# Turning stage and recurrence as one stage, and an expert stage that loads its own outputs

## What is computed

```
h = layernorm(x)
h = h + attention(layernorm(h))          # 16 heads
h = h + experts(layernorm(h))            # 8 experts, each token goes to the best one
x = x + 0.5 * h

z = layernorm(x)                         # no weights
dxa = shifted_by_one_token(z) - z
xm  = z + dxa * miu_x
lora = tanh(xm @ A_lora)
w_in, k_in, v_in, r_in, g_in = z + dxa * (lambda + lora @ B_lora)      # five mixes
k, v, r = k_in @ Wk.T, v_in @ Wv.T, r_in @ Wr.T;  g = silu(g_in @ Wg.T)
w = td_miu + tanh(w_in @ td_A) @ td_B;  decay = exp(-exp(w))
S_t = decay_t * S_(t-1) + k_t v_t;  y_t = r_t (S_(t-1) + u k_t v_t)    # per head
x = x + (groupnorm(y) * g) @ Wo.T

x = x + 0.5 * (the same attention-and-experts block applied to layernorm(x))
```

## Time and profile before

| | us |
|---|---|
| median of 3 runs (lowest to highest) | 1484.05 (1483.67 to 1486.18) |
| the profiled execution, its own time | 1485.67 |
| span of that execution, first to last instruction | 1483.3 |
| VectorE busy | 1059.5 (71%) |
| ScalarE busy | 870.2 (59%) |
| GpSimd busy | 637.5 (43%) |

### The profile page before, as it was taken

The page is one execution under the profiler, slowest core; times in us unless marked ns, Lnnn a source line. Parts: engine busy times, 40 slices in busy tenths (PEclk is TensorE's granted clock), DMA queues, the critical chain, the costliest instruction groups (busy, mean ns, idle before and its releaser), DMA issues. The chain is left out here.

```text
span 1483.3 us, 39412 instructions
## 1 busy us (share of the span) xinstructions
PE 1245.7 (84%) x12592; PEld 705.4 (48%) x12593; DVE 1059.5 (71%) x1888; ACT 870.2 (59%) x1726; POOL 637.5 (43%) x733
## 2 busy tenths in 40 slices
PE   5699999999968496398898747799999999784893
PEld 3333334343358496144455444333433333284893
DVE  7789999999555232478888748899999999173232
ACT  5288888888821253444335325388888888620451
POOL 4313433344337464356766533324323433447462
PEclk9799999999965698599999858799999999965897
DMA  5513432221001221100000005311111111002124
GB/s 161 188 46 80 110 100 64 52 57 48 12 1 40 59 67 55 37 2 3 4 3 2 3 1 194 102 49 57 48 54 48 56 46 44 2 10 63 53 65 124
DMA packets 81640, 81.93 MB, mean 55 GB/s; under 512 B 16265, under 2 KB 53868, under 8 KB 81536
## 3 DMA queue, kind: packets, MB, share of 16 engines
q1 hardware_dynamic: 72704, 70.01, 17.1%
q0 software_dynamic: 4608, 8.44, 1.7%
q10 hardware_dynamic: 4224, 2.10, 0.5%
HBM read 50.56 MB, written 29.93 MB: 54 GB/s over the span
## 5 line engine op out<-in xcount | busy, mean ns | idle before, releaser
L868 DVE TENSOR_REDUCE maxima<-ps 128x2 f32<-128x1024 f32 x512 | 624.0, 1226 | 53.5 <-PE ps L701 43.9
L854 ACT ACTIVATE probs<-ps 128x512 f32<-128x512 f32 x1024 | 551.7, 596 | 77.6 <-PE ps L728 60.8
L701 PE MATMUL ps<-k_stack,q_stack 62*128 62x512 f32 x1024 | 388.4, 474 | 17.5 <-DVE maxima L868 11.1
L728 PE MATMUL ps<-q_stack,k_stack 64*128 64x512 f32 x1024 | 382.4, 460 | 0.1
L739 PE MATMUL ps<-probs,v_stack 128*32 128x256 f32 x4096 | 327.6, 392 | 1.3 <-ACT probs L854 1.2
L701 PEld LDWEIGHTS ps<-k_stack,q_stack 62*128 62x128 f32 x1024 | 157.9, 192 | 218.1 <-DVE maxima L868 132.7
L657 POOL TENSOR_TENSOR inv<-o_rows,minus_one 128x32 f32<-128x32 f32 x32 | 174.2, 5444 | 29.5 <-ACT o_rows L835 29.5
L728 PEld LDWEIGHTS ps<-q_stack,k_stack 64*128 64x128 f32 x1024 | 161.9, 186 | 13.2 <-ACT probs L854 6.6
L649 POOL CAST neg_wide<-maxima 128x16 fp32r<-128x16 f32 x64 | 12.6, 196 | 349.8 <-DVE maxima L868 349.8
L739 PEld LDWEIGHTS ps<-probs,v_stack 128*32 128x32 f32 x4096 | 81.0, 108 | 170.4 <-issue 121.9
L1348 POOL DMA_INDIRECT expert_out<-yt,number x80 | 78.2, 978 | 69.1 <-POOL number L1344 32.1
(11 more groups left out here) (204 smaller groups left out, 1686.6 us busy)
## 6 DMA issues: line engine op xcount, KB each, us to landing
q_stack<-q_split SPq DMA_DIRECT2D x256, 64.0 KB
k_stack<-k_split SPq DMA_DIRECT2D x512, 32.0 KB
q_split<-q_parts SPq DMA_DIRECT2D x16, 512.0 KB, 3.2
k_split<-k_parts SPq DMA_DIRECT2D x16, 512.0 KB, 4.2
xt<-sorted SPq DMA_DIRECT2D x80, 64.5 KB
w<-in_L_ffn_w SPq DMA_DIRECT2D x16, 256.0 KB, 3.0
rows<-expert_out SPq DMA_DIRECT2D x16, 256.0 KB, 4.3
x_all<-in_L_attn_x SPq DMA_DIRECT2D x8, 256.0 KB, 3.0
```

Source lines behind the costliest of these rows:

```text
L701: mm = t.matmul(psS[:, h, :], qs[g][score_rows(h), h // 2, u * P:(u + 1) * P], ks[g][score_rows(h), h // 2, :], start=True, stop=True)
L728: t.matmul(ring("e", u, n), ks[g][half(h), h // 2, u * P:(u + 1) * P], qs[g][half(h), h // 2, :], start=True, stop=True).then_inc(e_ready, 1)
L854: a.activation(probs[u % 2][:, h, :], ring("e", u, n), ACT.Exp, scale=float(DK) ** -0.5).then_inc(e_read, 1)
L868: v.tensor_reduce(maxima[i][:, :, pair, u:u + 1], psS[:, 2 * pair:2 * pair + 2, :], AX_X, ALU.max, negate=True).then_inc(s_read, 1)
```

## The change

The expert stage's SyncE, after its last load, waits for the scatters of all four rings and issues the eight loads of `ys` itself, inside the expert stage. The semaphores that count these loads now belong to the program, one set for each of the two blocks. The combining stage only adds and stores.

```diff
+                for i in range(RING):
+                    sp.wait_ge(y_stored[i], 16 * (SLOTS // RING))
+                for j in range(SL):
+                    here = slice(j * ST, (j + 1) * ST)
+                    sp.dma_start(y_all[:, here, :], tiles_of(ys)[:, here, :]).then_inc(y_loaded[j], 16)
```

```diff
+            @block.sync
+            def _(sp):
                 for x in signals:
-                    pool.sem_inc(x.sem, 1)
...
+                    sp.sem_inc(x.sem, 1)
+                sp.sem_inc(opened, 1)
...
+                v.tensor_scalar(s["gn_w_half"][:], s["gn_w"][:], 0.5, None, ALU.mult).then_inc(halved, 1)
+                v.tensor_scalar(s["gn_b_half"][:], s["gn_b"][:], 0.5, None, ALU.mult).then_inc(halved, 1)
+                add(0)
+                for j in range(STARTED):
+                    moments_of(j)
+                vec.wait_ge(halved, 2)
...
                 def next_xm(b, i):
+                    if isinstance(b, int) and b <= 2:
+                        vec.wait_ge(kept, b + 1 if b < 2 else SL)
...
+                        if opening(b):
+                            moments_of(STARTED + f)
...
                 def scan_start(b, i):
+                    if opening(b):
+                        vec.wait_ge(stores_set, 2 + len(state))
```

On GpSimd the constants and the 14 factor memsets come first, then three roots, then the zeros of the five tiles; a root follows each of batch 0's mixes:

```diff
+                gn.start(pool)
+                for x in q_factor + k_factor:
+                    g.memset(x[:], 1.0).then_inc(factors_set, 1)
+                pool.wait_ge(constants, 2)
...
+                for j in range(STARTED):
+                    root(j)
+                for x in [diag, aT] + state:
+                    g.memset(x[:], 0.0).then_inc(stores_set, 1)
...
+                        if opening(b):
+                            root(STARTED + f)
```

On ScalarE a slice's activations and the copy of the slice before follow a part of batch 0; on TensorE a turn does:

```diff
+                def further(b, j):
+
+                    if opening(b):
+                        apply(j)
+                        keep(j - 1)
+
+                apply(0)
+                apply(1)
+                keep(0)
+                apply(2)
+                keep(1)
...
                     a.activation(lora4[:], ps[0:LORA, 1, :], ACT.Tanh).then_inc(lora_kept.sem, 1)
+                    further(b, 3)
...
                 def mix_chain(b, i):
+                    if opening(b):
+                        keep(SL - 1)
+                        act.wait_ge(factors_set, 2 * LEVELS)
...
+                for j in range(STARTED):
+                    turn(j)
...
+                def turn_at(b, part):
+                    if opening(b):
+                        turn(STARTED + ("td", "rate", "k", "r", "g").index(part))
```

More of the change, by code:

```diff
@@ L1353, in _, with combine_phase @@
                     pool.wait_ge(y_stored[i], 16 * (SLOTS // RING))
-def combine_phase(nc, x_all, y_all, ys, out):
+def combine_phase(nc, x_all, y_all, y_loaded, out):
     with Phase(nc) as ctx:
-        y_loaded = [ctx.semaphore(f"y_loaded{j}") for j in range(SL)]
         added, stored = ctx.semaphore("added"), ctx.semaphore("stored")
@@ L1408 @@
 GN_EPS = 1e-5 * NH
[L1411 to L1488, removed]
-                    act.wait_ge(turned, j + 1)
-                    a.activation(zT[:, j:j + 1, 1:], ps[:, j % 2:j % 2 + 1, :], ACT.Copy).then_inc(kept, 1)
-                for j in range(SL):
-                    act.wait_ge(shift_ready, j + 1)
-                    if j >= 2:
-                        act.wait_ge(turned, j - 1)
-                    for q in range(ST):
-                        last = a.activation(normed[j % 2][:, q, :], x_all[:, j * ST + q, :], ACT.Identity,
-                                            bias=shift[j % 2][:, q:q + 1], scale=rstd[j % 2][:, q:q + 1])
-                    last.then_inc(normed_ready, 1)
-                    if j >= 1:
-                        keep(j - 1)
-                keep(SL - 1)
-            @block.tensor
-            def _(pe):
-                for j in range(SL):
-                    pe.wait_ge(normed_ready, j + 1)
-                    if j >= 2:
-                        pe.wait_ge(kept, j - 1)
-                    for q in range(ST):
-                        last = nc.tensor.transpose(ps[:, j % 2, q * P:(q + 1) * P], normed[j % 2][:, q, :], s["ident"][:])
-                    last.then_inc(turned, 1)
@@ L1880, in _, with turn @@
                 t = nc.tensor
+                def turn(j):
+                    pe.wait_ge(normed_ready, j + 1)
+                    if j >= 2:
+                        pe.wait_ge(kept, j - 1)
+                    for q in range(ST):
+                        last = t.transpose(ps[:, TURN_BANK + j % 2, q * P:(q + 1) * P], normed[j % 2][:, q, :], s["ident"][:])
+                    last.then_inc(turned, 1)
+                for j in range(STARTED):
+                    turn(j)
                 def project(b, bank, weights, f, made, rows=P):
@@ L1986, in scan_keys @@
                     k_next.wait(pe, b, LEVELS)
+                    if opening(b):
+                        pe.wait_ge(kept, SL)
                     x_added.free(pe, b)
@@ L2072, in ffn @@
             project_phase(nc, ps, s, x_all, z_all, rows, expert, first_row, xs)
-            expert_phase(nc, ps, s, expert, first_row, xs, ys)
-        ffn(load)
+            expert_phase(nc, ps, s, expert, first_row, xs, ys, y_all, y_loaded)
+        y_loaded = [[ctx.semaphore(f"y_loaded{n}_{j}") for j in range(SL)] for n in range(2)]
+        ffn(y_loaded[0], load)
         with ExitStack() as inner:
             zT = inner.enter_context(nc.sbuf_tensor("zT", [P, B, T + 1], F32))
-            turn_phase(nc, ps, s, x_all, y_all, ys, zT)
-            recurrence_phase(nc, ps, s, x_all, zT)
-        ffn()
-        combine_phase(nc, x_all, y_all, ys, out)
+            recurrence_phase(nc, ps, s, x_all, y_all, y_loaded[0], zT)
+        ffn(y_loaded[1])
+        combine_phase(nc, x_all, y_all, y_loaded[1], out)
 _INS = ['L0_attn_x', 'L0_ffn_w_proj', 'L0_ffn_ln1_w', 'L0_ffn_ln1_b', 'L0_ffn_ln2_w', 'L0_ffn_ln2_b',
```

102 lines of the change are left out of this document (78 added, 24 removed).

## The result

The changed kernel takes 1473.74 us (median of 4 runs, 1473.05 to 1475.03) against 1484.12 before (4 runs, 1483.67 to 1486.18): ratio 0.9934, 95% interval 0.9906 to 0.9963. That is 0.7 above the forecast of 1473.0 and inside its range. The profiled execution took 1475.03, its span is 1473.1, 10.2 less than before.

What follows compares the result with a forecast made beforehand. The first seam was taken as bound by latency, then ScalarE as the opening's bound; 7.7 - 0.2 + 3.5 = 11.0 gained from a median of 1484.05 gave 1473.0 us, range 1467 to 1479.

Steps and rivals of the forecast that it cites:

- Loads at the first seam: Between expert stage and first add: SyncE's issuing replaces GpSimd's drain as what the barrier awaits; first add near 592.3, 0.2 lost.
- End: Last scatter to span's end: loads issued earlier, eight adds run without a wait, stores end sooner; 3.5 gained, ends 2.5 and 4.2.
- Opening: First add to batch 1's first shift: 20.4 saved up to batch 0's first shift, part paid back; 7.7 gained.
- the paying back: Between first shifts of batches 0 and 1: five late slices lengthen the stretch from 16.84 to 29.5.
- The step that makes ScalarE the bound: Inside batch 0, behind a head of 4.2: ScalarE sets the pace with 20.9 of work, plus waits.
- Low clock through the opening: Rival: TensorE stays at 0.50 through the opening, the path ends 4.3 later; 1477.4 us, chance 0.12.
- the argument against it: Against the low clock: from the shifts on TensorE has some 8 us of work without a gap.
- Contention: In the opening: late slices' two-input VectorE adds slow beside GpSimd's mix; stretch between first shifts 30.2 with it, 28.9 without.
- "The overlap itself brings nothing": Opening: batch 0 after the last slice without barriers would start its LoRA matmul near 615.5, 8.5 earlier; the gain is the seam's.
- SyncE's drain: Rival at the barrier: this drain waits for its loads' data, 2.8 lost at the opening, 1.0 gained at the end; 1478.2, chance 0.06.
- the five round trips: Rival in batch 0: late slices' trips between engines stand in series, costing 34; 1494, chance 0.05; partly in series 1484, 0.05.
- the signs named: Trace landmarks: LoRA matmul near 604, ScalarE hardly a gap 616 to 640, batch 1's first shift near 641, last loads near 1454.

Runs made afterwards that it cites:

- e11: The changed kernel with one activation instead of four for each of the five late slices, leaving work out; 1465.66 us, one execution.
- e12: The changed kernel with VectorE making statistics of one tile instead of four of each late slice, leaving work out; 1469.51 us, one execution.
- e4: The changed kernel with five loads issued in front of the barrier and three behind it, at both seams; 1469.71 us against 1485.26 before.
- e1: The changed kernel with all eight slices turned ahead of batch 0, the stages still merged; 1465.72 us against 1485.26 before.
- e2: The changed kernel with SyncE issuing the eight loads behind the barrier again, at both seams; 1472.63 us against 1485.26 before.

## Why the prediction was right, and where it was not

- **Loads at the first seam**, 0.2 lost: 0.3 gained. The mechanism was right to the row: SyncE's issuing took the place of GpSimd's drain, and the drain of SyncE is 0.12. The term missed mainly because the issues took 5.66 where 5.99 was put in. That number varies from 5.2 to 6.5 between executions. The first add at 591.64 lies 0.66 from the 592.3 named, a little outside the 0.5 that was allowed.
- **End**, 3.5 gained: 3.9 by the traces, and the adds ran without a wait as forecast. Right.
- **Opening**, 7.7 gained: 9.1. Of the difference 0.7 is a LoRA matmul 10.76 behind the first add instead of 11.5; 1.65 is the stretch from it to the first shift's end, 6.29 instead of 7.94, as the clock rose at 604.8, within that stretch and not behind it; and −1.0 is the paying back, 30.54 instead of 29.5. The step that makes ScalarE the bound held in the main (e11), with VectorE's work counting by less than half beside it (e12); ScalarE's waits were 4.84 instead of 3.4.
- **Low clock through the opening**, the first rival, came in part, and the argument against it failed. TensorE did not have 8 us of work without a gap: it waited 2.15 for a shift that had queued behind a late slice's moments on VectorE. 0.50 was granted from 611.7 to 625.3, and the matmul pairs of 2.1 behind 616, named as a sign of being wrong, are there (2.07 at 616.92). The wait alone does not explain the fall, as e4 has the same wait at 1.00. And it cost 1.0 to 1.3, not 4.3: the 4.3 was for 0.50 through the whole opening. That ScalarE's work hid some of it is likely, and not shown.
- **Contention** was there but struck other instructions. The term was put on the late slices' adds; one of four was slowed (1.11 against 0.67), which began 0.52 behind a mix of the usual 1.09. The other three were recorded within 0.04 of a mix's start and took 0.67 or 0.68, and those mixes took 1.64 or 1.65 instead of 1.09. The scaling behind such an add (613.40, 0.65 instead of 0.17) then ends at 614.05, with the mix (614.03). The Trainium skill, SBUF — State Buffer, in Who interferes with whom, states that one instruction at a time holds the ports that VectorE and GpSimd share, that the order of issue decides which of the two blocks, and that VectorE's `tensor_scalar` can take them in its two-port modes. The slowed add and the scaling agree with this; for the other three adds the records do not show the order of issue, as they put the mix 0.02 to 0.04 ahead of an add that was not slowed. The prediction used the sentence on two inputs alone, without the order.
- **"The overlap itself brings nothing"** is the step that failed. It costs 3.6 to 4.9, of which 1.0 to 1.3 is the clock's. The prediction set a LoRA matmul without overlap at 615.5, or 23.4 behind the first add; in e1 it is 20.85, because VectorE makes batch 0's `dxa` and `xm` while ScalarE and TensorE are still at the last slices, and the matmul does not need the last copy. From there to the end of batch 0's first shift e1 takes 6.50 instead of 7.94, as the clock rose within that stretch (0.72 granted from 610 to 615). It then counted the same ScalarE work in both places. In front a slice costs 2.02, as ScalarE has no gap; behind, the same work costs 2.8, with 4.84 of waits, 3.73 of them for products that queue behind turns. ScalarE's 5.75 of idle time ahead of its first late slice is not used either, since that slice has to come through VectorE and GpSimd first.
- **The rest.** SyncE's drain waited for no data, and the five round trips did not stand in series (30.54, not some 50). Of the signs named, the LoRA matmul came at 602.40 for 604, batch 1's first shift at 639.23 for 641, the last loads at 1455.21 for 1454. ScalarE did not run from 616 to 640 with hardly a gap: it waited 4.4 by 633.7. That the sum of 11.0 stands so close to 10.2 in the traces is luck: the three terms gave 13.3, and 3.3 went in the stretch that scatters.

## What to carry to other kernels

Price a merged stage and an overlap apart: here merging the stages earned all of the opening's gain, and interleaving the leftover work with the next batch gave 3.6 to 4.9 of it back, because ScalarE is the pace in both places and waits more in one of them. Interleave only where the bounding engine has idle time that the work can reach in time. When transfers are issued ahead of a barrier, count the issuing time of those that nobody needs at once; five in front and three behind was 2.3 better than eight at the first seam, and no better at the end.

## What the runs showed of the hardware

- Five loads of 256 KB were issued in 2.59, eight in 5.2 to 6.5, so the last three took as long as the first five or longer (in the changed kernel's trace 2.59 and 3.07).
- GpSimd's drain behind its scatters took 3.33 at 585.0, SyncE's 0.12 right behind eight issued loads, the last of them issued less than 0.2 earlier, while a load's data came 2.8 behind its issue (e2): that drain does not wait for data.
- After one and the same wait of TensorE's, 2.15 ahead of batch 0's first decay product, the granted clock fell from 1.00 to 0.50 within 0.6 in the changed kernel's two traces, and stayed at 1.00 in e4.
- Two executions of one kernel differed by 4.7 in 810 us of equal work, more than most of the terms argued about here; the openings of the same two differed by 0.3, those of the changed kernel's two traces by 0.9.
